# First mixture: rows stored as they lie and gathered per routed tile, in place of a scatter into slots

## The reference, cut to what matters

```
logits = relu(xf @ Wr1 + br1) @ Wr2 + br2           # 2048 tokens, 8 experts
gates  = softmax(logits); tg, ti = top_k(gates, 2); tg = softmax(tg / 2)
out    = silu(xf @ Ws1 + bs1) @ Ws2 + bs2           # the shared expert, every token
for e in range(8):
    h   = silu(xf @ We1[e] + be1[e]) @ We2[e] + be2[e]
    out = out + sum(tg * (ti == e))[:, None] * h    # only the two chosen count
```

## Time and profile before

| | us |
|---|---|
| median of 3 runs | 880.41 |
| lowest, highest | 877.93, 883.48 |
| the profiled execution's own time | 882.07 |
| its span | 880.1 |
| PE busy | 813.7 (92%) |
| DVE busy | 662.6 (75%) |
| ACT busy | 474.5 (54%) |
| POOL busy | 249.1 (28%) |

### The profile page before, as it was taken

How to read it: one execution, slowest core, us unless ns; L and a number is a source line. 1 busy time by engine, 2 the same in 40 slices (tenths; PEclk the granted TensorE clock), 3 DMA queues, 4 the chain that set the end, 5 groups by cost and what they waited for, 6 DMA issues and landing times. The chain is left out here.

```text
span 880.1 us, 17731 instructions
## 1 busy us (share of the span) xinstructions
PE 813.7 (92%) x6055; PEld 756.6 (86%) x6055; DVE 662.6 (75%) x1356; ACT 474.5 (54%) x1004; POOL 249.1 (28%) x212
## 2 busy tenths in 40 slices
PE   8999999996999959999999999998899878999977
PEld 6887999996699959999999999995788845889877
DVE  4986999996795435888888888976887778876657
ACT  3653233232465537777777777753455542645553
POOL 8411332331005640022433333230122201532540
PEclk9998999998899979999999999997899989999999
DMA  8980000000404237577777767823000051534325
GB/s 301 300 220 1 1 0 1 0 1 4 152 1 133 103 125 286 205 223 233 239 239 237 227 214 220 293 25 102 1 0 1 0 181 33 172 103 125 105 93 178
DMA packets 55794, 111.72 MB, mean 127 GB/s; under 512 B 8306, under 2 KB 41684, under 8 KB 48948
## 3 DMA queue, kind: packets, MB, share of 16 engines
q1 hardware_dynamic: 44148, 93.29, 31.9%
q0 software_dynamic: 9408, 15.53, 7.2%
q10 hardware_dynamic: 2176, 2.10, 0.8%
HBM read 82.19 MB, written 28.70 MB: 126 GB/s over the span
## 5 line engine op out<-in xcount | busy, mean ns | idle before, releaser
L143 PE MATMUL e_ps_h<-e_xh,e_w1h 128*128 128x256 f32 (+1 forms) x496 | 141.4, 285 | 0.0
L144 PE MATMUL e_ps_h<-e_xl,e_w1h 128*128 128x256 f32 (+1 forms) x496 | 138.9, 280 | 0.0
L145 PE MATMUL e_ps_h<-e_xh,e_w1l 128*128 128x256 f32 (+1 forms) x496 | 138.5, 279 | 0.0
L2179 POOL DMA_INDIRECT accumulated<-m_yo,m_token x39 | 72.9, 1869 | 198.3 <-ACT m_yo L2320 172.4
L143 PE MATMUL e_ps_o<-e_w2h,e_hh 128*128 128x256 f32 x440 | 122.4, 278 | 0.0
L144 PE MATMUL e_ps_o<-e_w2l,e_hh 128*128 128x256 f32 x440 | 121.9, 277 | 0.0
L145 PE MATMUL e_ps_o<-e_w2h,e_hl 128*128 128x256 f32 x440 | 121.9, 277 | 0.0
L2300 ACT ACTIVATE e_hf<-e_ps_h,e_b1s 128x256 f32<-128x256 f32 (+1 forms) x248 | 98.0, 446 | 36.8 <-PE e_ps_h L145 36.8
L1064 POOL TENSOR_TENSOR at_pr<-at_pr,at_inv 128x1168 f32<-128x1168 f32 (+2 forms) x48 | 58.6, 1235 | 204.3 <-DVE at_inv L901 204.3
L144 PEld LDWEIGHTS e_ps_h<-e_xl,e_w1h 128*128 128x128 f32 x496 | 94.6, 191 | 0.0
L143 PEld LDWEIGHTS e_ps_h<-e_xh,e_w1h 128*128 128x128 f32 x496 | 94.6, 191 | 0.0
(11 more groups left out here) (425 smaller groups left out, 2277.4 us busy)
## 6 DMA issues: line engine op xcount, KB each, us to landing
e_w1s<-in_m_w SPq DMA_DIRECT2D x24, 1024.0 KB, 4.8
e_w2s<-in_m_w SPq DMA_DIRECT2D x24, 1024.0 KB, 7.1
slots_in<-zero SPq DMA_DIRECT2D x20, 258.0 KB, 9.4
e_xin<-slots_in SPq DMA_DIRECT2D x16, 258.0 KB, 4.8
last_slots_in<-zero SPq DMA_DIRECT2D x14, 258.0 KB, 8.8
d_xin<-last_slots_in SPq DMA_DIRECT2D x10, 258.0 KB, 2.8
d_results<-last_results SPq DMA_DIRECT2D x10, 256.0 KB, 5.5
as_wk<-in_a_wk SPq DMA_DIRECT2D x2, 1024.0 KB, 9.1
```

The source lines that it names most:

```text
L143: nc.tensor.matmul(out, lh, rh, start=start, stop=False)
L144: nc.tensor.matmul(out, lh, rl, start=False, stop=False)
L145: return nc.tensor.matmul(out, ll, rh, start=False, stop=stop)
L2179: nc.gpsimd.indirect_dma_start(out=g.acc, out_offset=bass.IndirectOffsetOnAxis(ap=token[:, n, a:a + 1], axis=0), in_=yo[:, q, a, :], in_of ...
```

## The change: what it does

Both copies of the rows (one with the first gate, one with the second) are stored to DRAM in token order by two plain transfers of SyncE, to a buffer `choices_in` of 2 x 2048 rows and 256 filler rows. After the slot numbers are known, VectorE builds for each choice a 0/1 matrix of the position in the block and one of the block (`places`). TensorE multiplies them (`invert`, 32 products of 128 x 120) between step 3 and step 4. VectorE turns the result into a table of 40 columns with the source row of every row of every tile (`source`). GpSimd then fetches a tile's rows with one or two indirect transfers (`gather`), tiles n = 0, 1 and 2 ahead of the loop and tile n + 3 within it. The scatter, SyncE's row loads and 19 of 20 zeroing transfers are gone.

The core of the diff:

```diff
     def zero_slots(self, sp):
-        for a in range(0, rows.shape[1], 2):
-            sp.dma_start(rows[:, a:a + 2, :], self.g.zero[:]).then_inc(self.g.s_zeroed, 16)
+        sp.dma_start(rows, self.g.zero[:]).then_inc(self.g.s_zeroed, 16)
...
+    def places(self, dve, i):
...
+        v.tensor_tensor(self.at[i].rearrange("p (t x) -> p t x", t=NT), wide(self.iota_pos, P), pos[:].to_broadcast([P, NT, P]),
+                        ALU.is_equal).then_inc(self.s_at, 1)
+        v.tensor_tensor(of[:, :, 0, :], wide(self.iota_unit, COLS), base[:].to_broadcast([P, NT, COLS]), ALU.is_equal).then_inc(self.s_at, 1)
+        dve.wait_ge(self.s_at, 4 * i + 2)
+        v.tensor_scalar(of[:, :, 1, :], of[:, :, 0, :], self.iota_p, None, ALU.mult).then_inc(self.s_at, 1)
...
+        v.scalar_tensor_tensor(out=of[:, :, 2, :], in0=turn, scalar=float(i * NT), in1=of[:, :, 0, :],
+                               op0=ALU.add, op1=ALU.mult).then_inc(self.s_at, 1)
+    def invert(self, pe, ps_i):
+        pe.wait_ge(self.s_at, 4 * TOPK)
+        for i in range(TOPK):
+            for t in range(NT):
+                last = self.nc.tensor.matmul(ps_i, self.at[i][:, t * P:(t + 1) * P], self.of[i][:, t].rearrange("p c u -> p (c u)"),
+                                             start=i == t == 0, stop=(i, t) == (TOPK - 1, NT - 1))
+        last.then_inc(self.s_inv, 1)
+    def source(self, dve, ps_i):
...
+        dve.wait_ge(self.s_inv, 1)
+        v.tensor_copy(got, ps_i).then_inc(self.s_got, 1)
+        dve.wait_ge(self.s_got, 1)
...   (four small linked instructions)
+        v.tensor_copy(self.m.rows[:], row).then_inc(self.s_rows, 1)
...
     def slots(self, dve, between):
...
-            v.tensor_copy(m.slots[:, i, :], self.mx[:, :, 0]).then_inc(self.s_k, 1)
+            link(dve, v.tensor_copy(whole, self.mx[:]))
+            link(dve, v.tensor_scalar(whole, whole, -P, None, ALU.bitwise_and))
+            link(dve, v.tensor_copy(base[:], whole))
+            link(dve, v.tensor_tensor(pos[:], self.mx[:], base[:], ALU.subtract))
...
-def scatter(nc, g, m, router, pool, s_gate):
...
     def gpsimd(pool):
+        def gather(n):
+            q = n % 2
+            if n >= 2:
+                pool.wait_ge(s_xlo, S + n - 1)
+            for a in range(rows_of(S + n)):
+                col = 2 * n + a if n < PAIRS else PAIRS + n
+                nc.gpsimd.indirect_dma_start(
+                    out=xin[:, q, a, :], out_offset=None, in_=g.xs,
+                    in_offset=bass.IndirectOffsetOnAxis(ap=m.rows[:, col:col + 1], axis=0)).then_inc(s_xl[q], 16)
         router.gpsimd(pool)
-        scatter(nc, g, m, router, pool, s_gate)
+        pool.wait_ge(router.s_gated, 1)
+        pool.wait_ge(s_src, 16)
+        nc.gpsimd.tensor_copy(m.xn[:, :, GATE], router.gates[:, 1, :]).then_inc(s_gate, 1)
...
+        pool.wait_ge(s_src, 32)
+        pool.wait_ge(router.s_rows, 1)
+        for n in range(3):
+            gather(n)
         pool.wait_ge(s_acc, 16 * S)
         for n in range(ROUTED):
             q = n % 2
+            if n + 3 < ROUTED:
+                gather(n + 3)
...
             pool.wait_ge(s_ys, n + 1)
             if n:
                 pool.wait_ge(s_st[1 - q], stored(n - 1))
...   (the one or two indirect stores of tile n, as before)
     def sync(sp):
...
-                wait(sp, s_xlo, j - 1)
...
-                    sp.dma_start(xin[:, q], rows).then_inc(s_xl[q], 16)
...
+        for i in range(TOPK):
+            if i:
+                sp.wait_ge(s_gate, i)
+            else:
+                sp.wait_ge(router.s_gated, 1)
+                sp.wait_ge(router.s_ids, 1)
+            sp.dma_start(g.xs[i * TOK:(i + 1) * TOK].rearrange("(t p) d -> p t d", p=P), m.xn[:]).then_inc(s_src, 16)
         sp.wait_ge(router.s_eid, 1)
         step(S, S % 2)
+        sp.wait_ge(s_src, 16 * TOPK)
+        sp.wait_ge(s_xlo, S - 1)
         early.load(sp)
...
     def tensor(pe):
...
         for j in range(2, S + 1):
             make(True)(j, j % 2)
+            if j == 3:
+                pe.wait_ge(s_ev, 2)
+                router.invert(pe, ps_i)
+                pe.wait_ge(router.s_got, 1)
...
     def vector(dve):
...
-        steps(dve, make(True), 2, S + 1, (3, S - 1))
+        router.places(dve, 0)
+        make(True)(2, 0)
+        router.places(dve, 1)
+        make(True)(3, 1)
+        router.source(dve, ps_i)
+        steps(dve, make(True), 4, S + 1, (4, S - 1))
```

More of the change, by code:

```diff
@@ L1827, in __init__ @@
         self.s_sf, self.s_ed, self.s_num = sem(T + "gate_difference"), sem(T + "gate_exp"), sem(T + "numbered")
-        self.s_k, self.s_eid = sem(T + "slots"), sem(T + "tile_experts")
+        self.s_gated, self.s_eid = sem(T + "gated"), sem(T + "tile_experts")
+        self.s_at, self.s_inv = sem(T + "places"), sem(T + "inverted")
+        self.s_got, self.s_rows = sem(T + "inverse_copied"), sem(T + "rows")
         self.s_w, self.s_xn, self.s_t = sem(T + "weights"), sem(T + "xn"), sem(T + "transposed")
@@ L1845, in staging, with inverse @@
             self.hid, self.lg = sb("hid", [RH, 2, CT * P]), sb("biased_logits", [P, NT, E])
+    def inverse(self, w1h, w1l, w2h, w2l, w2s):
+        n = NT * 3 * COLS
+        self.at = [a[:, 1, :] for a in (w1h, w1l)]
+        self.of = [a[:, 1, 0:n].rearrange("p (t c u) -> p t c u", t=NT, c=3) for a in (w2h, w2l)]
+        self.iota_pos, free = w2s[:, 1, 0:P], w2s[:, 1, P:]
+        self.iota_unit, self.none = free[:, 0:COLS], free[:, COLS:2 * COLS]
+        self.iota_t, self.iota_p = free[:, 2 * COLS:2 * COLS + NT], free[:, 2 * COLS + NT:2 * COLS + NT + 1]
@@ new lines, in invert @@
+    def invert(self, pe, ps_i):
[6 more added lines that the diff above has]
+    def source(self, dve, ps_i):
+        v, link = self.nc.vector, self.chain.link
+        flat = lambda a: a[:].rearrange("p t e -> p (t e)")
+        got, row, gap = flat(self.ex)[:, 0:3 * COLS], flat(self.pro)[:, 0:COLS], flat(self.pro2)[:, 0:COLS]
+        dve.wait_ge(self.s_inv, 1)
+        v.tensor_copy(got, ps_i).then_inc(self.s_got, 1)
+        dve.wait_ge(self.s_got, 1)
+        link(dve, v.scalar_tensor_tensor(out=row, in0=got[:, 2 * COLS:], scalar=float(P), in1=got[:, COLS:2 * COLS], op0=ALU.mult, op1=ALU.add))
+        link(dve, v.tensor_scalar(gap, got[:, 0:COLS], -1.0, 1.0, ALU.mult, ALU.add))
+        link(dve, v.tensor_tensor(gap, gap, self.none, ALU.mult))
+        link(dve, v.tensor_tensor(row, row, gap, ALU.add))
+        v.tensor_copy(self.m.rows[:], row).then_inc(self.s_rows, 1)
@@ L1859, in gpsimd @@
                             allow_small_or_imprecise_dtypes=True).then_inc(self.s_ids, 1)
-        pool.wait_ge(self.s_ids, 1)
+        for dst, pattern, base, each in (
+                (self.iota_pos, [[1, P]], 0, 0), (self.iota_unit, [[P, COLS]], 0, 0), (self.iota_t, [[1, NT]], 0, 0),
+                (self.iota_p, [[0, 1]], 0, 1), (self.none[:, 0:2 * PAIRS], [[0, PAIRS], [P, 2]], TOPK * TOK, 1),
+                (self.none[:, 2 * PAIRS:], [[0, COLS - 2 * PAIRS]], TOPK * TOK, 1)):
+            self.nc.gpsimd.iota(dst, pattern=pattern, base=base, channel_multiplier=each,
+                                allow_small_or_imprecise_dtypes=True).then_inc(self.s_ids, 1)
+        pool.wait_ge(self.s_ids, 7)
     def tensor(self, pe, between):
@@ L2535, in build @@
         sb = lambda name, shape, dt=FP: ctx.enter_context(nc.sbuf_tensor(f"m{L0.n}_{name}", shape, dt))
-        m.slots, m.eid = sb("slots", [P, TOPK, NT], I32), sb("tile_expert", [1, L0.tiles + 1], I32)
+        m.rows, m.eid = sb("rows", [P, COLS], I32), sb("tile_expert", [1, L0.tiles + 1], I32)
         m.token, m.gate = sb("token", [P, ROUTED, ST // P], I32), sb("gate", [P, ROUTED, ST // P])
@@ L2544, in build @@
         deviations.append(SplitDeviation(nc, g, sem, f"m{L1.n}_ln"))
-        m.s_sc = [sem(f"m{L0.n}_scattered{q}") for q in range(2)]
         with ExitStack() as mix:
@@ L2559, in build @@
             done.remove(h)
-        done = [h for h in done if h not in (g.s_zeroed1, *m.s_sc, *m.s_st)]
+        done = [h for h in done if h not in (g.s_zeroed1, *m.s_st)]
         done = [h for h in done if h not in (deviations[1].s_v, deviations[1].s_q, deviations[1].s_r)]
```

32 lines of the change are left out of this document (17 added, 15 removed).

## The result

The changed kernel takes 1055.45 us (median of 4 runs, 1049.07 to 1059.06). The kernel before took 879.17 beside it (4 runs, 877.48 to 883.48). The ratio is 1.199, with an interval of 1.191 to 1.207: some 176 us slower. The forecast was 1022, the range 966 to 1075, and slower had 0.96. Direction and mechanism came as forecast, and the forecast loss was 34 us too small (142 against 176).

The account below looks back on a forecast made before the run. The prediction saw a 9.4 us TensorE stall for the scatter's slots and GpSimd's in-order queue as decisive: 882.1 - 5 (opening) + 147 (loop) = 1024 us against the profile, 1022 against the median; range 966 to 1075.

Parts of the forecast that it names:

- The step that decides: GpSimd's queue in the loop: gather(n + 3) stands behind a store waiting for scaling, so steps stall; loop +147 us.
- not slower, the gathers are hidden anyway: Rival for the loop: gathers issued early enough to be hidden, only the opening's -5 left; 876 us, chance 0.04.
- The store's place: GpSimd's store in a pair step: begins at +9.0 us, plus 2.0 for the low clock after each stall.
- the second gather, 2.6 from issue to landing: Last term of the pair step's chain: 2.6 us, as the scatter, after a 0.3 gap, ending at +19.5.
- the 96: Pair steps, starts of steps 11 to 22: +8.0 us each over 11.5, twelve times.
- the cast holds the gathers up wholly: Rival: a gather beside VectorE's cast loses up to 1.2 us, not 0.6; 11 us more, 1033 us, chance 0.08.
- Tile 11: Start of step 10: its gather waits for the last shared store and lands at 365.6 against 363.5, +2 us.
- The singles: Starts of steps 23 to 29, single tiles with one gather: +5.7 to +8.9 us each, together 47.
- The clock term of 2.0: Steps after a stall: the low clock makes the store begin 2.0 us later in each step's chain.
- The light chain: Rival: the clock doesn't fall at each stall, 20 x 2.0 us less; 982 us, chance 0.15.
- The heavy chain: Rival: gathers land as the adding stores do, 4.6 us later, 92 more; about 1114 us, chance 0.10.
- The opening: Stretch before tile 8: 6.5 us added by index work, 11.7 removed with the scatter's stall and slow clock; -5.

Follow-up runs that it names:

- lead of four: Changed kernel with four tiles gathered ahead of the loop and gather(n + 4) within it: 884.09 us against 881.20 for the kernel before, ratio 1.0035.
- lead of five: Changed kernel with five tiles gathered ahead of the loop and gather(n + 5) within it: 879.09 us against 882.26 for the kernel before, ratio 0.997.
- rounding kept away: Changed kernel with VectorE waiting, from step 10 on, for the gathered rows before it rounds the weights: 1032.47 us, ratio 1.1722.
- clock held up: Changed kernel with 11 products of zeros on TensorE ahead of each wait for gathered rows from step 9 on: 1025.2 us, ratio 1.161.
- the gathers ahead of the stores: Changed kernel with the gather of tile n + 4 behind the wait for tile n's scaling but ahead of its store: 962.96 us, ratio 1.0923.

## Why the prediction was right, and where it was off

*The step that decides was right.* "Three ahead" is less than one step ahead, since the gather stands behind a store that waits for ScalarE. The lead of four takes nearly all of the loss away, and the lead of five all of it, with the same gathers and stores. The rival "not slower, the gathers are hidden anyway" gave the cure in words (one more tile of lead), and the runs show that one tile is nearly enough and two are enough.

*The store's place was right:* +9.0 and 2.0 for the clock gives +11.0, and the trace has 11.0 and 10.6. The two stores took 3.5 us for 3.7. The second gather's start was met in the long kind of step (+16.9 in step 16) and lay 1.2 us earlier in the short one (+15.7 in step 17).

*The term that was off in the pairs is the last one, "the second gather, 2.6 from issue to landing".* It is 4.7 in the long kind of step and 3.5 in the short one. The prediction gave 0.6 to VectorE's cast beside the first gather and nothing to the low parts of w2 and w1 right behind it, into which the second gather falls. The first gather can be long as well: it took 1.8 to 1.9 us where the cast began during it, and the forecast had 1.57. With the rounding kept away the landing is 2.8, 0.2 over the scatter's that was taken. Against the 96 the pairs gave 106.8, and 87.5 (225.9 - 138.4) with the rounding kept away. The forecast without its twelve times 0.6 would be 88.8. So the chain was sized right, and this one term wasn't.

A gather that starts inside VectorE's cast or low part ends some 0.85 us after it. The rival "the cast holds the gathers up wholly" was right about the cast. Its price for VectorE, 19 x 1.2 = 23 us, is also what the experiment gave (19 + 4), but that is luck: it put a whole cast beside each first gather, and what cost the time was the second gather in the cast or in the low part behind it, which the rival didn't name. It is not enough for the measured time either (1033 against 1055). The Trainium skill (SBUF — State Buffer, "Who interferes with whom") gives a cast as an instruction that can hold the port pair it shares with GpSimd, and says of a subtraction with both inputs in SBUF that it contends with a GpSimd instruction that reads SBUF, while it infers that descriptor generation isn't held by it. The trace agrees on the cast (1.56 to 1.79 against 0.97 us). It is against the inference: here the subtraction held an indirect gather, whose row numbers lie in SBUF, just as well, up to 2.83 us.

*Tile 11.* Forecast +2, measured +5.6. Its gathers began at 358.4 and 359.9, which is +10.0 and +11.6 of step 9. The forecast's 359.25 + 2.5 is +9.7 of its step 9 (from 352.0), and 1.3 more for the second, so they were 0.3 and 0.5 late. But they landed after 5.4 and not 2.6 us. SyncE's two 1 MB weight loads had gone out at 355.8 and 356.9. The "quiet DMA engines" of the forecast hold from step 10 on only. With the lead of five nearly all gathers meet such loads: 6.7 us of landing in the median, near the heavy end (7.2), and hidden by the lead.

*The singles.* Forecast +47, measured +59. Counted by the step that each start closes: the starts of steps 23 and 24 came after 16.9 and 17.5 us (forecast 18.2), those of 25 and 26 after 19.8 and 22.3 (17.2), those of 27 to 29 after 17.4, 16.5 and 16.2 (14.8). The clock term of 2.0 failed here: in step 25 the store began at +13.1 and not at +8.8, since the clock was at 0.50 for over 12 us. With the clock held up two of the last steps take 13.2 each. Why the slow clock lasts so much longer in these steps is open.

*The light chain* (982) is refuted for the pairs, where the clock fell at every stall. Its argument that a fall wasn't to be taken for granted has something to it, though. The forecast held against it that no stall would be shorter than 3.8 us; five of the twenty were (1.51 to 3.75), and after one of them, in front of step 29, the clock stayed at 1.00. The experiment with the gathers ahead of the stores has more such cases, 3.56 us in front of its step 16 among them.

*The heavy chain* (1114, gathers landing as late as adding stores) is refuted for this kernel, 3.4 against 7.2 in the median. It would be nearer the truth for gathers beside the loads (5.4 to 6.7).

*The opening* gave -6.1 where -5 was forecast. The stall went, and step 7 came down to 11.5. Of the +6.5, 5.65 came (step 3 took 17.18 us). The wait among step 3's first products was 1.4 rather than 2.4, and the one for the copy 0.4 rather than 0.6. The zeroing transfers at the start were worth nothing, as taken. The +2.4 ahead of step 0 isn't the change's: in the eight traces that share the changed code up to there step 0 starts anywhere from 240.23 to 243.26, and before it was at 240.27.

Taken together, the sum was 29 us short against the trace (142 for 171): 3.6 at tile 11, 10.8 in the pairs, 12 in the singles and 4 before step 0 and behind step 29, less the 1 that the opening gave more. The chain itself held; its last gather and, in the singles, its clock term were sized too small.

## What to carry to other kernels

A prefetch that is issued by an engine with other work is ahead by what stands behind it in that engine's queue, not by the number in its index. Count the steps to the wait it stands behind, and put it ahead of that wait or make the lead larger.

Where a DMA is issued by GpSimd in a chain that sets the step, look at what VectorE does in those few microseconds. The weights' rounding beside it cost more here (23 us) than the whole opening gained.

Once a step has a stall, price the slow clock after it from a row of the same shape of work: a pair step paid 1.5 to 2.0 us for it and a single one at least 2.3 in the mean.

## What the runs showed of the hardware

- Indirect gathers of 128 rows took 0.97 and 1.02 us to issue with nothing of VectorE's beside them. In the changed kernel they took 1.56 to 1.79 when started inside its 128x2048 cast, and 2.75 to 2.83 early inside its 128x2048 subtraction with both inputs in SBUF, and ended 0.83 to 0.89 us after that instruction.
- The same gather lands after 2.8 us on quiet DMA engines, 5.4 just behind two 1 MB loads, and 6.7 in the median under the full flow of the lead of five, where the adding stores before took 7.2.
- After a stall of 5.69 us TensorE ran at 1.2 GHz for 4.1 us in a pair step (step 16), and after one of 2.47 us for over 12 us in a single one (step 25), though it was busy throughout in both. After 1.72 us of stall the clock fell only once TensorE was busy again (step 27), and after 2.78 us it stayed at 2.4 GHz (step 29).
- An f32 product of 256 columns against the identity cost 0.43 us at the full clock (10.35 us for 24, 4.7 for 11), so that filling a hole of 5 us takes 11 of them.
